# Masked outputs seated evenly over the column tiles, four heads' records stored ahead, and rotary pieces every ninth slot

## The reference

```python
def masked(x, Wqkv, bqkv, Wo, bo):               # stage 0
    q, k, v = heads(x @ Wqkv + bqkv)
    att = einsum('bhqd,bhkd->bhqk', q, k) / sqrt(8)
    att = where(i[None, :] >= i[:, None], att, -inf)    # a key at or behind its query
    return einsum('bhqk,bhkd->bhqd', softmax(att), v) @ Wo + bo
def rbf(...):    # stage 1: exp(-dist2 * r_sigma) @ v, no softmax
def rel(...):    # stage 2: softmax with shifted relative positions
def rotary(...): # stage 3: rope(q), rope(k), then plain softmax attention
x = x + masked(layernorm(x)); x = x + ffn(layernorm(x))
x = x + rbf(layernorm(x));    x = x + ffn(layernorm(x))
x = x + rel(layernorm(x));    x = x + ffn1(layernorm(x))
x = x + rotary(layernorm(x)); x = x + ffn1(layernorm(x))
```

## Time and profile before

| | us |
|---|---|
| median of 3 runs | 2823.63 (2823.32 to 2838.18) |
| profiled execution, its own time | 2820.36 |
| span of the profile | 2818.6 |
| up to the first masked exponential | 53.5 |
| masked, from 65 to 571 | 506 |
| radial (571 to 1062), relative (1062 to 2070) | 491, 1008 |
| rotary, from about 2070 to 2785, and the end | 715, 34 |

### The profile page before, as it was taken

One profiled execution on the slowest core, in us unless ns is written; L12 is line 12 of the kernel. 1 busy time (PEld: TensorE's weight loads), 2 busy tenths in 40 slices (PEclk: granted clock), 3 DMA queues, 4 the chain that ended last, 5 costly groups with the idle time before them and its releaser, 6 DMA issues.

```text
span 2818.6 us, 107129 instructions
## 1 busy us (share of the span) xinstructions
PE 2662.6 (94%) x43752; PEld 1600.2 (57%) x43752; DVE 2070.0 (73%) x5519; ACT 2103.6 (75%) x3769; POOL 898.3 (32%) x1604
## 2 busy tenths in 40 slices
PE   5999999999999999999999999999999999999996
PEld 3666665655555555666666666666644444444444
DVE  6788888722222228888788888878889989999993
ACT  3677776799999996666666666666677878878874
POOL 2212223321303242622541361252135144351321
PEclk7999999999999999999999999999999999999998
DMA  3534232433423342411321241222123123232221
GB/s 113 152 100 118 81 115 80 116 119 113 127 88 121 104 147 57 133 53 57 93 88 50 73 131 50 74 81 70 46 64 107 56 71 98 66 98 68 68 72 32
DMA packets 197218, 250.16 MB, mean 89 GB/s; under 512 B 48292, under 2 KB 113124, under 8 KB 196728
## 3 DMA queue, kind: packets, MB, share of 16 engines
q1 hardware_dynamic: 195288, 241.21, 28.9%
q10 hardware_dynamic: 1440, 2.10, 0.2%
HBM read 132.89 MB, written 100.07 MB: 83 GB/s over the span
## 4 chain that ended last, share of the span: by engine, by line
PE 69%; DVE 20%; issue 5%; ACT 2%; DMA 1%; SPq 1%; POOL 0%; ACTq 0%; DVEq 0%; POOLq 0%
PE ppv L1010 29%; DVE mx L1311 14%; PE ring L867 6%; PE ring L917 6%; PE ring L852 5%; PE ring L878 4%; PE ring L950 3%; PE pm L1050 2%; DVE seen L1295 2%; DVE seen L1306 1%; ACT probs L1167 1%; PE ring L966 1%; PE pm L1035 1%; PE pm L1113 1%; PE pm L1104 1%
## 5 line engine op out<-in xcount | busy, mean ns | idle before, releaser
L1167 ACT ACTIVATE probs<-ring 128x512 f32<-128x512 f32 (+1 forms) x3280 | 1970.1, 682 | 647.0 <-PE ring L867 316.0
L1311 DVE TENSOR_REDUCE mx<-ring 128x1 f32<-128x512 f32 (+2 forms) x2112 | 1284.9, 651 | 226.6 <-PE ring L917 89.3
L1010 PE MATMUL ppv<-probs,values 128*32 128x128 f32 x30208 | 1147.3, 278 | 7.5 <-POOL probs L1590 3.1
L1010 PEld LDWEIGHTS ppv<-probs,values 128*32 128x32 f32 x30208 | 793.1, 109 | 320.1 <-issue 162.9
L1306 DVE CUSTOM_DVE_ANT_0 seen<-ring,low_seen 128x512 f32<-128x512 f32 x576 | 392.9, 682 | 71.8 <-PE ring L917 71.5
L924 PE MATMUL ring<-kst,qst 48*128 48x512 bf16 (+1 forms) x1060 | 361.6, 390 | 34.8 <-DMA kst<-records_k 17.4
L878 PE MATMUL ring<-qst,kst 51*128 51x512 bf16 (+2 forms) x1092 | 345.5, 384 | 4.5 <-ACT probs L1167 3.6
L1560 POOL CAST mparts<-mall 128x8 bf16<-128x8 f32 x192 | 37.0, 193 | 827.6 <-DVE mall L1329 700.8
L917 PE MATMUL ring<-kst,qst 112*128 112x512 bf16 (+3 forms) x768 | 251.5, 328 | 11.8 <-DVE mx L1295 6.7
L1590 POOL TENSOR_SCALAR_AFFINE_SELECT probs<-probs 128x512 f32<-128x512 f32 x128 | 81.6, 638 | 564.0 <-ACT probs L1167 351.3
L867 PE MATMUL ring<-qst,kst 115*128 115x512 bf16 (+3 forms) x768 | 250.9, 327 | 0.0
(11 more groups left out here) (170 smaller groups left out, 3001.9 us busy)
## 6 DMA issues: line engine op xcount, KB each, us to landing
qst<-records_q SPq DMA_DIRECT2D x448, 96.0 KB
heads_out<-osb SPq DMA_DIRECT2D x256, 128.0 KB, 2.0
kst<-records_k SPq DMA_DIRECT2D x320, 96.0 KB
records_k<-parts SPq DMA_DIRECT2D x96, 256.0 KB, 3.2
records_q<-parts SPq DMA_DIRECT2D x90, 256.0 KB, 3.4
kst<-records_k SPq DMA_DIRECT2D x128, 102.0 KB
oT<-heads_out SPq DMA_DIRECT2D x60, 128.0 KB, 2.7
proj<-proj SPq DMA_DIRECT2D x96, 64.0 KB, 2.0
```

Of the source, the lines that this page charges most:

```text
L1010: mm = pe.matmul(ppv[32 * g:32 * g + 32, c:c + P], values[:, (n // H) % 2, v:v + 32], src[:, at * P:(at + 1) * P], start=u == 0 and qt < 4 ...
L1167: nc.scalar.activation(probs_of(rd.n, u), src, ACT.Exp, scale=1.0 if rd.s == RBF else SCALE).then_inc(s_exp, 1)
L1311: ins = dve.tensor_reduce(mx[:, slot, to:to + 1], bank[:, at * P:(at + nt) * P], AX.X, ALU.max)
```

## The change

Four edits stand in it.

1. **Seats.** Query tiles 4 to 7 of the masked stage are seated in column tiles 3, 2, 1, 0 in place of 0, 1, 2, 3, and the single tiles (4, 4) and (0, 0) trade units. Each unit now has its four tiles in four column tiles. The output projection reads its columns by the same seats.
2. **First records.** Of sequence 0 the rows of heads 0 to 3 are stored first, from both queues, with a semaphore of their own; the other twelve heads follow, from SP behind the loads of three heads, from ScalarE before its first exponential.
3. **Constants.** Fourteen loads move from SP to ScalarE's queue, at the start, once the first x has landed. The rest stays on SP, every fourth tick from round 3; weights and tables of the last two stages get a semaphore that is waited for at round 96. The memset of `values` moves from VectorE to GpSimd.
4. **Pieces.** `APART` of the rotary intervals goes from 6 to 9.

```diff
 KQ_UNITS = {
-    MASKED: [[(7, 0, 4, 0)], [(7, 4, 4, 0)], [(6, 0, 4, 0)], [(6, 4, 3, 0), (4, 4, 1, 3)], [(5, 0, 4, 0)],
-             [(5, 4, 2, 0), (1, 0, 2, 2)], [(4, 0, 4, 0)], [(3, 0, 4, 0)], [(2, 0, 3, 0), (0, 0, 1, 3)]],
+    MASKED: [[(7, 0, 4, 0)], [(7, 4, 4, 0)], [(6, 0, 4, 0)], [(6, 4, 3, 0), (0, 0, 1, 3)], [(5, 0, 4, 0)],
+             [(5, 4, 2, 0), (1, 0, 2, 2)], [(4, 0, 4, 0)], [(3, 0, 4, 0)], [(2, 0, 3, 0), (4, 4, 1, 3)]],
+def seat(s, qt):
+    g = 3 - qt % 4 if s == MASKED and qt >= 4 else qt % 4
+    return g, qt // 4 * P
-APART = {MASKED: 3, RBF: 6, REL: 3, ROPE: 6}
+APART = {MASKED: 3, RBF: 6, REL: 3, ROPE: 9}
...
-                if n % H == 0:
+                if n == 0:
+                    sp.wait_ge(s_r0, 16 * STORES[0])
+                elif n == EARLY or n % H == 0:
                     sp.wait_ge(s_rec, records_to(n // H))
...
-                tick = ROUNDS[1].tick
+                tick = ROUNDS[3].tick
...
-                    tick += 2
+                    tick += 4
...
             for n in range(3):
                 load(n)
+            for e in range(6):
+                sp.dma_start(records_k[EARLY:H, e * D:(e + 1) * D], parts[EARLY * D:P, 0, KPARTS6[e]]).then_inc(s_rec, 16)
...
-                    g, c = qt % 4, qt // 4 * P
+                    g, c = seat(rd.s, qt)
...
                             q = (2 * t + h) * P
+                            g, c = seat(s, 4 * h + t)
+                            q = 2 * P * g + c
...
-                            act.dma_start(records_q[0:H, e * D:(e + 1) * D], parts[:, 1, QPARTS6[e]]).then_inc(s_rec, 16)
+                            act.dma_start(records_q[0:EARLY, e * D:(e + 1) * D], parts[0:EARLY * D, 1, QPARTS6[e]]).then_inc(s_r0, 16)
...
+            act.wait_ge(s_x[0], 16)
+            for dst, src in [(t[:, 1], a["L0_attn_b_Wqkv"][:, n * C:(n + 1) * C]) for n, t in enumerate((wq, wk, wv))] + \
...
+                act.dma_start(dst, src).then_inc(s_c3, 16)
```

More of the change, by code:

```diff
@@ L509, in build @@
         s_half = sem("s_half")
+        s_vset = sem("s_vset")
+        s_r0 = sem("s_r0")
+        s_c2 = sem("s_c2")
+        s_c3 = sem("s_c3")
         s_cm = sem("s_cm")
@@ L607, in const_rows @@
                 for slot in range(SLOTS):
[L608 to L614, removed]
+                    sp.dma_start(keys[ROW + BASE:ROW + BASE + 3, slot], k["minus3"].bitcast(BF16)).then_inc(s_kc[s], 16)
                     if s == REL:
@@ L748, in others @@
                     load_x(b)
-                for n, t in enumerate((wq, wk, wv)):
-                    yield later()
[L751 to L761, removed]
+                yield later()
+                const1(wcand, a["L0_ffn_W"].rearrange("e c n -> c e n"))
+                yield later()
+                const1(bcand, a["L0_ffn_b"].rearrange("(o e) n -> o e n", o=1).to_broadcast([P, NOPS, C]))
+                for s, (w, bias) in ((2, ("L1_attn_a_Wo", "L1_attn_a_bo")), (3, ("L1_attn_b_Wo", "L1_attn_b_bo"))):
+                    yield later()
+                    const1(wo[:, s], a[w])
+                    yield later()
+                    const1(bo[:, s], rowb(a[bias]))
+                assert tick < ROUNDS[H - 1].tick
+                for c in (0, ROW):
+                    for slot in range(SLOTS):
+                        yield later()
+                        sp.dma_start(kst[1][c + BASE + 3:c + BASE + 6, slot], k["ones3"].bitcast(BF16)).then_inc(s_kc[RBF], 16)
+                        yield later()
+                        sp.dma_start(qst[1][c + BASE:c + BASE + 3, slot], k["ones3"].bitcast(BF16)).then_inc(s_kc[RBF], 16)
+                small = []
                 for s, n in ((2, "L1_attn_a"), (3, "L1_attn_b")):
@@ L772, in others @@
                     yield later()
-                    const1(dst, src)
-                yield later()
-                const_rows(RBF)
-                assert tick < ROUNDS[H - 1].tick
+                    const2(dst, src)
+                assert tick < ROUNDS[REL_WORK - H].tick
             load_x(0)
@@ L1008, in take_values @@
                     if rd.s == MASKED:
-                        last = u == 7 and qt == 3 or u == 8 and (kt, qt) in ((0, 0), (2, 1), (2, 2))
+                        last = final
                     mm = pe.matmul(ppv[32 * g:32 * g + 32, c:c + P], values[:, (n // H) % 2, v:v + 32],
@@ L1121, in _ @@
             pe.wait_ge(s_set, SETS)
-            pe.wait_ge(s_dset, 3)
+            pe.wait_ge(s_dset, 2)
             pe.wait_ge(s_q0, 4)
@@ L1264, in _ @@
             nc.scalar.activation(pick[:, 8, 0:1], pick[:, 7, 0:1], ACT.Ln).then_inc(s_ac, 1)
+            for e in range(6):
+                act.dma_start(records_q[EARLY:H, e * D:(e + 1) * D], parts[EARLY * D:P, 1, QPARTS6[e]]).then_inc(s_rec, 16)
             for rd in ROUNDS.values():
+                if rd.n == REL_WORK:
+                    act.wait_ge(s_c2, NC2[0])
                 for u in range(rd.slots):
@@ L1403, in starts @@
                         dve.memset(work[:, :, :], 0.0).then_inc(s_dset, 1)
-                        dve.memset(values[:, :, :], 1.0).then_inc(s_dset, 1)
                     if on_vector(j):
@@ L1770, in _ @@
             pool.memset(qst[0][:, :, :], 0.0).then_inc(s_set, 1)
+            pool.memset(values[:, :, :], 1.0).then_inc(s_vset, 1)
             pool.wait_ge(s_half, 1)
```

42 lines of the change are left out of this document (35 added, 7 removed).

## The result

The changed kernel took 2788.07 us (median of four runs, 2783.55 to 2803.82) beside 2823.48 for the kernel before: a ratio of 0.9869, 95% interval 0.9828 to 0.991. The forecast was 2785, between 2766 and 2804. The kernel ran again among the experiments: 2801.41 (five runs, 2799.89 to 2805.82), ratio 0.9919 [0.9905, 0.9932]. So its own executions differ by as much as some terms of my sum; both medians lie in the range. The profiled execution took 2803.82, its span 2801.5; it is the longest of the four.

A forecast was written before the change was run, and what follows sets the result against it. TensorE, busy 94%, was taken as the main bound, but in plain masked rounds it and VectorE take turns. Terms 21.8 + 5.5 + 6.0 + 6.0 = 39.3 us off 2820.36 gave 2781, plus 3.3 for the median: 2785, range 2766 to 2804.

The forecast's parts named there:

- Seats: Masked stage: `ppv` groups at 0.79 us each save 0.62 TensorE time a head, of which 21.8 us comes through.
- A plain round becomes 7.02 - 0.24 = 6.78 us: Plain masked rounds: only VectorE's 0.24 gap closes, its 0.45 gap stays; 32 x 0.24 = 7.7 us.
- The walk: Plain masked round followed from VectorE's unit 6: TensorE runs ahead, its 0.44 wait for a bank grows; round 6.78, not 6.40.
- First records: Start: smaller first stores are issued and land earlier, first exponential at 48; 5.5 us, between 3.6 and 6.6.
- Six at 0.46 ... and I let it land in 2.7: First stores: last issued at about 28.4, 3.6 us earlier, landing in 2.7 in place of 4.66.
- Constants: Interval 0: nearly all 9.4 us lost come back, less 3.4 for a stall in rounds 21 and 22; 6.0 net.
- Rotary: Rotary intervals: pieces nine slots apart instead of six shorten VectorE's waits; 6.0 us, between 0 and 9.2.
- Nine slots win back 0.66 and leave 0.39, 0.22 less: Rotary pieces: TensorE catches up 0.66 of a piece's 1.05 us, so VectorE waits 0.39, 0.22 less than with six.
- TensorE's time whole: Rival: VectorE's 0.45 gap closes too, every masked round gives 0.62; 39.7 in place of 21.8, 2767 us; chance 0.14.
- Tables stall and spacing nothing: Rival: stores and tables of rounds 21 and 22 cost 9.4, the rotary term is 0; 2797 us; chance 0.13.
- Seats nothing: Rival: `ppv` groups differ by order or size of weights, not seats; 17.5 us less gain, 2806; chance 0.06.
- slower: Rival: odd-slot pieces make VectorE wait 0.65 more for each of 42 pieces, +27 us; about 2839; chance 0.05.

The follow-up runs named there:

- Seats alone: Kernel before with the new seats (memset of `values` on GpSimd) and nothing else of the change: 2805.94 us, ratio 0.993 to before.
- all but the seats: Changed kernel with the old seats: 2814.0 us, ratio 0.9956 to before.
- old gathers: SyncE's gathers of a finished interval timed as in the changed kernel; a run starting them 4, 7 or 6 slots later took 2788.27 us, 0.987.
- six apart on odd slots: Changed kernel with rotary pieces six slots apart instead of nine, all on odd slots: 2791.17 us, ratio 0.9888 to before.
- Constants as before: Changed kernel with all constants issued on SP again, every second tick from round 1: 2803.77 us, ratio 0.9928 to before.

## Why the prediction came out right, term by term

**Seats: forecast 21.8, measured 20.8 by stage and 22.3 by medians, but not made up as I had it.** Seats alone against before: 24 plain rounds give 12.7 (0.53 each), 25 others 10.0, the six rounds of the constants 2.0, rounds 21 and 22 0.6, and rounds 16, 31, 32, 47, 48 and 51, in which intervals meet, take 4.6 back. The forecast had 7.7 in plain rounds and 14.1 in 32 others. By class: TensorE-bound 0.59 (forecast 0.62), normalising 0.57 (0.45), statistics 0.14 to 0.34 (0.15), plain 0.55 where I said 0.24.

The step that failed is "A plain round becomes 7.02 - 0.24 = 6.78 us". It takes the 6.33 us of VectorE outside its two gaps for work. A merged row of the timeline, three reductions from 281.64 in 1.56 us, hides a third wait. Before, and then after:

```profile
281.05 1.28 DVE L1311 TENSOR_REDUCE mx<-ring 128x1 f32<-128x512 f32 x2
282.45 0.56 DVE L1311 TENSOR_REDUCE mx<-ring 128x1 f32<-128x384 f32 x1
```

```profile
261.53 0.68 DVE L1351 TENSOR_REDUCE mx<-ring 128x1 f32<-128x512 f32 x1
262.13 0.55 DVE L1351 TENSOR_REDUCE mx<-ring 128x1 f32<-128x384 f32 x1
```

Before, VectorE ends unit 2 at 282.33 and starts unit 3 at 282.45, 0.12 later. After, unit 3 starts at 262.13, 0.08 before the record of unit 2 ends at 262.21: where no wait parts them, records of neighbouring instructions overlap by 0.08. So this place gives 0.20. The place I did count gives 0.24 and the same overlap, 0.32. The two make 0.52 of the 0.55. The walk also read the row "282.48 0.44 issue" as TensorE's wait for a bank, and forecast that it would grow to 0.6 or more. The row lies within VectorE's unit 3. TensorE's own idle is 0.30 there and did not grow, since unit 3 now comes earlier; before, and then after:

```profile
283.26 0.28 PE L960 MATMUL ring<-kst,qst 48*128 48x256 bf16 x1 [0.30 <-DVE mx L1311]
```

```profile
262.93 0.28 PE L981 MATMUL ring<-kst,qst 48*128 48x256 bf16 x1 [0.28 <-DVE mx L1351]
```

In the plain round of now VectorE's `mx` is 77.3% of the chain. The Trainium skill (TensorEngine Tiling (Array Packing), section PSUM Bottleneck) says that tiling doesn't speed up what empties PSUM; the trace agrees about the end point, a round of 6.47 that VectorE sets, and I had put that point 0.3 too high.

That 20.8 met 21.8 is in part chance. Outside the six rounds in which intervals meet, the seats give 25.4 (seats alone against before) and 25.8 (the changed kernel against all but the seats). The 4.6 of the six rounds can't be laid on the seats: they sum to 56.1 in the kernel before, to 61.2 in the one with all but the seats and to 57.8 to 67.6 in those with the new seats and the old gathers, with a granted clock of 0.66 in one of the changed kernel's. Gathers ahead of the placing are one cause (31, 47), shown above; why they grew against before was not settled.

**First records: forecast 5.5, measured about 1.2.** "Six at 0.46 ... and I let it land in 2.7" failed: a quarter of the bytes is issued in 0.60 to 1.26 us each and lands in 3.93 (1.51 and 4.66 before). From the first store's issue to the sixth's it is 4.8 us in place of 5.9, so the issues give 1.1 and the landing 0.7. The load of head 0's keys on the chain then lands in 3.35 in place of 2.75, which takes 0.6 back. The six stores of the other heads on ScalarE's queue begin at 35.27, just ahead of that load (36.32); that they slow it is likely and was not tested. From the first store to the first exponential it is 26.2 us in place of 27.4. The first exponential came at 52.39, not 48. The cover for the constants on ScalarE's queue held.

**Constants: forecast 6.0, measured 5.4 to 8.0.** Rounds 5 to 10 give 9.3 between seats alone and the changed kernel (49.5 to 40.2; 41.5 when it ran again), and rounds 21 and 22 cost 1.3 (2.1) instead of 3.4. Against the kernel that differs in the constants alone it is 7.4 (5.4). The DMA share there is 0.94, and the placing takes 3.24 us, not 6.22. The 3.4 was no bad guess for all that: rounds 21 and 22 took 19.0 in the profile of six apart on odd slots, where seats alone took 13.5. Constants as before are 24.5 under before by medians and the changed kernel 35.4 or 24.6: they can't size the term.

**Rotary: forecast 6.0, measured 3.8 where no clock fell.** It is 1.4 in each of three intervals, and 0.4 lost in the last. In the changed kernel's own profile the third interval gave nothing, because its longest round took 14.79 in place of 13.24, and a first round took 13.07 where it took 11.67 before, so the stage gave only 0.7. No round with three pieces is left; the forecast 12.5 has nothing to answer to, and the longest round, 13.23, ends on a value and an output piece. The step "Nine slots win back 0.66 and leave 0.39, 0.22 less" is not the ground: six slots apart on odd slots give the same fourteen rounds. What nine slots do is to land in slot 0 only once in these rounds, where six even slots land there three times.

The measured terms, 20.8 + 1.2 + 7 + 3.8, make about 33 against the forecast 39.3; the medians say 35 and 25. The forecast of 2785 was nearer to the first median than its terms were to theirs: the start and the spacing were put too high, the second median is 16 above it, and that 2788 came out beside 2785 is in part luck. The rivals: *TensorE's time whole* came nearer than I gave it credit for, a plain round gives 0.55 of 0.62. *Tables stall and spacing nothing*: the stall is 1.3 to 5.6 and the spacing 3.8. *Seats nothing* and *slower* are refuted by the plain rounds and by the odd slots.

What stays open: why an idle of 1.28 us brings the clock down in six profiles and not in eight, and for 3.4 us or for 51. The place, the change from wide to narrow exponentials in the radial stage, was not edited.

## What to carry to other kernels

When two engines take turns, a stretch of one engine without shown idle isn't all work: compare its busy sum with the stretch, and read the single instructions behind merged rows, before using it as a floor. In an in-order DMA queue the short transfer that the next round needs must be ahead of bulk issues; each change of spacing moves these too, so look at the queue at every rerun. Once a kernel is near its bound, long single instructions and queue stalls cost more than their length, because TensorE's clock may fall behind them: cutting one reciprocal in four gave a median of 2783 where the changed kernel, measured at other times, had 2788 and 2801. Before an early mark such as the first copy is used as a measure, look whether the granted clock rose before or after it.

## What the runs showed of the hardware

- Column tiles: with three of twelve tiles in each, the group takes 0.79 to 0.84, as the line through 3, 4 and 5 tiles said.
- Stores of a quarter of the bytes were hardly cheaper: 0.60 to 1.26 us to issue, 3.93 to land.
- VectorE's records of neighbouring reductions overlap by 0.08 us, and a wait between them costs that on top of what it shows.
- TensorE at 1.2 GHz for 34 us while it was shown busy for all of each 4 us, after an idle of 1.28; a group of 16 `ppv` took 1.08 us there. Radial stages of the 14 profiles: seven at 525.2 to 525.3, one of 526.6 without a fall, and the six with one 526.8 to 547.6.
